# Attention and feed-forward layer on eight cores: the feed-forward moved a step later, a sequence's last halves of Q, K and V put beside its own attention, first loads in pieces, one span projected at first

## The reference, cut to what matters

```python
q, k, v = proj_heads(x, w_q), proj_heads(x, w_k), proj_heads(x, w_v)
scores = einsum('bhqd,bhkd->bhqk', q, k) / sqrt(64) + causal_mask
out = einsum('bhqk,bhkd->bhqd', softmax(scores), v)
x = layernorm(x + out @ w_o.T)
x_prev = x shifted by one token
xr = mu_r * x + (1 - mu_r) * x_prev
xk = mu_k * x + (1 - mu_k) * x_prev
ffn = sigmoid(xr @ W_r.T) * (square(relu(xk @ W_k.T)) @ W_v.T)
y = layernorm(x + ffn)
```

## Time and profile before

| | |
|---|---|
| median of 3 runs (lowest to highest) | 1367.66 us (1366.4 to 1368.92) |
| the profiled execution, whole | 1365.98 us |
| its span on the slowest core (of 8: 1347.0 to 1364.4) | 1364.4 us |
| TensorE busy | 1229.6 us, 90% |
| ScalarE, VectorE, GpSimd busy | 726.9 (53%), 653.4 (48%), 325.4 (24%) us |
| mean granted TensorE clock, as a share of 2.4 GHz | 0.975 |
| DMA: software queue (GpSimd), hardware queue (SP), share of 16 engines | 31.0%, 15.7% |

### The profile page before, as it was taken

How to read it: one execution, slowest core, us unless ns; L and a number is a source line. 1 busy time by engine, 2 the same in 40 slices (tenths; PEclk the granted TensorE clock), 3 DMA queues, 4 the chain that set the end, 5 groups by cost and what they waited for, 6 DMA issues and landing times.

```text
span 1364.4 us, 45398 instructions; the slowest of 8 cores (1347.0 to 1364.4 us)
## 1 busy us (share of the span) xinstructions
PE 1229.6 (90%) x18870; PEld 607.7 (45%) x18884; DVE 653.4 (48%) x1126; ACT 726.9 (53%) x1004; POOL 325.4 (24%) x440
## 2 busy tenths in 40 slices
PE   3999899989999598999997999999999969799776
PEld 1445354544454244444563545454444524344343
DVE  0005565456635164243275355636672615714696
ACT  1346555364656468666343254656565566877221
POOL 1002224211520115311124311631153110530141
PEclk9999999999999899999997999999999999999989
DMA  9977267964224722228643364345422471322302
GB/s 156 236 197 190 69 162 165 245 193 145 79 76 157 204 78 73 74 77 246 204 151 92 125 206 163 117 135 186 154 94 87 138 228 59 125 76 79 125 32 93
DMA packets 52617, 187.34 MB, mean 137 GB/s; under 512 B 11584, under 2 KB 27840, under 8 KB 36032
## 3 DMA queue, kind: packets, MB, share of 16 engines
q0 software_dynamic: 16416, 119.54, 31.0%
q1 hardware_dynamic: 36000, 64.89, 15.7%
HBM read 159.49 MB, written 31.46 MB: 140 GB/s over the span
## 4 chain that ended last, share of the span: by engine, by line
PE 74%; DMA 8%; DVE 5%; SPq 4%; ACT 4%; issue 3%; POOL 2%; DVEq 0%; POOLq 0%; ACTq 0%
PE DB L342 50%; PE S L709 9%; PE PVb L750 8%; SPq L820 4%; ACT P L724 4%; DMA rb<-rec 4%; PE DEN L773 3%; PE S L342 2%; DMA y<-x 2%; PE DB L507 2%; DMA ring<-wq 1%; DVE rec L812 1%; DMA ring<-wkf 1%; POOL QO L828 1%; POOL tmp L521 0%
## 5 line engine op out<-in xcount | busy, mean ns | idle before, releaser
L724 ACT ACTIVATE P<-S 128x1024 bf16<-128x1024 f32 (+3 forms) x640 | 535.4, 899 | 167.2 <-PE S L709 167.0
L709 PE MATMUL S<-QO,Kt 64*128 64x512 bf16 (+3 forms) x1280 | 187.1, 353 | 34.6 <-ACT P L724 33.5
L342 PE MATMUL DB<-xT,ring 128*32 128x512 bf16 (+1 forms) x2686 | 182.8, 380 | 21.3 <-DMA ring<-wq 20.9
L750 PE MATMUL PVb<-P,Vt 128*32 128x512 bf16 (+3 forms) x2560 | 179.0, 356 | 6.2 <-DVE u_s L810 3.7
L828 POOL TENSOR_TENSOR QO<-u_s,rb 128x512 bf16<-128x512 f32 x63 | 82.0, 1301 | 409.0 <-DMA rb<-rec 348.8
L734 DVE TENSOR_TENSOR P<-P,tri_s 128x512 bf16<-128x512 bf16 x128 | 63.7, 500 | 221.9 <-ACT P L724 221.8
L342 PE MATMUL DB<-ring,kact 128*32 128x512 bf16 x2312 | 143.9, 383 | 5.0 <-issue 2.8
L342 PE MATMUL DB<-ring,QO 128*32 128x512 bf16 (+1 forms) x1822 | 115.4, 387 | 22.9 <-POOL QO L828 20.8
L342 PEld LDWEIGHTS DB<-xT,ring 128*32 128x32 bf16 (+1 forms) x2688 | 97.0, 97 | 83.2 <-issue 25.5
L262 POOL DMA_DIRECT2D ring<-wscr x90 | 53.5, 594 | 336.1 <-PE S L709 184.2
L773 PE MATMUL DEN<-P,ones 128*32 128x256 bf16 (+1 forms) x2244 | 120.8, 270 | 8.5 <-DVE rec L812 8.4
(11 more groups left out here) (115 smaller groups left out, 1193.8 us busy)
## 6 DMA issues: line engine op xcount, KB each, us to landing
ring<-wscr POOLq DMA_DIRECT2D x90, 1024.0 KB, 6.5
rb<-rec SPq DMA_DIRECT2D x504, 32.0 KB, 2.9
x<-x SPq DMA_DIRECT2D x28, 512.0 KB, 8.7
wscr<-ring SPq DMA_DIRECT2D x14, 1024.0 KB, 10.1
y<-x SPq DMA_DIRECT2D x28, 512.0 KB, 7.6
xT<-xt POOLq DMA_DIRECT2D x6, 1024.0 KB, 12.5
ring<-wq POOLq DMA_DIRECT2D x2, 1024.0 KB, 25.5
kact<-xt POOLq DMA_DIRECT2D x2, 1024.0 KB, 18.6
```

What stands on the lines that cost most here:

```text
L342: mi = nc.tensor.matmul(out=b[r:r + w], lhsT=lhs[:, r:r + w], rhs=rhs, start=(cch == 0), stop=(cch == NCH - 1))
L709: mi = nc.tensor.matmul(out=sp[:, 512 * hh:512 * hh + n], lhsT=Kt[r, T * t + 128 * j:T * t + 128 * j + 128], rhs=QO[g % 2][r, SPW * t + q0 ...
L724: tok[("exp", k)] = SE.done(nc.scalar.activation(out=p3[:, :, 0:n], in_=s3, func=AF.Exp, bias=EXP_BIAS, scale=0.125), 0.14 + 2 * n / 1145)
L750: nc.tensor.matmul(out=PVb[r:r + 32, q0:SPW], lhsT=Vt[:, D * j + 128 * t + r:D * j + 128 * t + r + 32], rhs=P[:, p0 + h0:p0 + h0 + SPW - q ...
```

## The change

- `items_of` takes the place of `stages`. Step g now has F and RV of span g-2 (from step 2 on), then K of span g+1, O of g-1, Q of g+1, and T of g-1 in turns with V of g+1. Step 7 ends with F and RV of span 6.
- Of spans 3 and 7 only the first halves of K, Q, V (columns 0 to 511, pairs 0 to 3) are made in the step before; the last halves (`own_q`, `own_k`, `own_v`) are made in steps 3 and 7 beside the same span's attention. `s_unit` and `pv_unit` wait for K and V of the own span only on the diagonal.
- At first only span 0 is projected (`START`, 24 items: Q1 K1 K0 Q0 V0 V1), the halves K0, Q0, V0, V1 stay in the ring, and step 0 has span 1's 24 items.
- Dense items by step: 24 at first, then 24, 32, 44, 60, 8 (V of span 4 alone), 56, 56, 44, 68 and 32 behind.
- The first four half weights and xT of span 0 are loaded in four pieces of 512 KB of float32 each, with a semaphore for each piece; Q, K and F weights are laid out on the host so that a piece serves one item. `load_x` of span 0 waits until xT of span 0 has been read.
- Only span 1's xT lies in the kact tile; the others follow one another in the xT tile.
- `epilogue` copies on VectorE or ScalarE, whichever is free first; items are issued in halves in steps 3 and 7; some numbers of the planner change.

```diff
@@ -31,10 +31,10 @@
 NU = 3
 NB = 3
 LAG = 2
-XALT = (1, 5)
+XALT = (1,)
 DENSE = 1.75
 HALF = DENSE / 2
-AGE = 4.0
+AGE = 3.0
 class Ctr:
...
@@ -195,29 +197,44 @@
             return b
-        HALVES = {"K": [("wk", 0), ("wk", 1)], "Q": [("wq", 0), ("wq", 1)],
-                  "K0": [("wk", 0)], "K1": [("wk", 1)],
-                  "V": [("wv", 0), ("wv", 1)], "O": [("wo", 0), ("wo", 1)],
+        HALVES = {"K0": [("wk", 0)], "K1": [("wk", 1)], "Q0": [("wq", 0)], "Q1": [("wq", 1)],
+                  "V0": [("wv", 0)], "V1": [("wv", 1)], "O": [("wo", 0), ("wo", 1)],
                   "F": [("wkf", 0), ("wkf", 1)], "T": [],
                   "RV": [("wr", 0), ("wvf", 0), ("wr", 1), ("wvf", 1)]}
+        def items_of(g):
+            r, p, n = g - 2, g - 1, g + 1
+            def of(span, text):
+                return [(st, span) for st in text.split()]
+            def pairs(ts, side):
+                return [it for two in zip(ts, side) for it in two] + ts[len(side):] + side[len(ts):]
+            f, rv = (of(r, "F " * 8), of(r, "RV " * 16)) if r >= 0 else ([], [])
+            o, t = of(p, "O " * 8), of(p, "T " * 8)
+            k0, k1, q0, q1, v0, v1 = [of(n, st * 4) for st in ("K0 ", "K1 ", "Q0 ", "Q1 ", "V0 ", "V1 ")]
+            own_k, own_q, own_v = [of(g, st * 4) for st in ("K1 ", "Q1 ", "V1 ")]
+            if n == G:
+                return f + rv + own_q + o + pairs(t, own_k + own_v) + of(p, "F " * 8 + "RV " * 16)
+            if n % NSP == 0:
+                return f + own_q + rv + own_k + own_v + o + q0[:2] + pairs(t, q0[2:] + q1) + k0 + k1
+            if n % NSP == NSP - 1:
+                return f + rv + k0 + o + q0 + t[:2] + v0[:1] + t[2:4] + v0[1:2] + t[4:] + v0[2:]
+            return f + rv + k0 + k1 + o + q0 + q1 + pairs(t, v0 + v1)
         def stages(g):
-            p, n = g - 1, g + 1
-            if n == G:
-                return [("O", p), ("T", p), ("F", p), ("RV", p)]
-            if n % NSP == 0:
-                return [("O", p), ("Q", n), ("T", p), ("F", p), ("RV", p), ("K", n)]
-            if n % NSP == NSP - 1:
-                return [("K0", n), ("O", p), ("K1", n), ("T", p), ("V", n), ("F", p), ("RV", p), ("Q", n)]
-            first = [("K", n)] if g > 1 else []
-            return first + [("O", p), ("Q", n), ("T", p), ("V", n), ("F", p), ("RV", p)]
-        order = [("Q", 0), ("K", 0), ("V", 0), ("K", 2)]
+            return list(dict.fromkeys(items_of(g)))
+        START = ["Q1", "K1", "K0", "Q0", "V0", "V1"]
+        order = [(st, 0) for st in START] + [("K1", 1), ("Q1", 1)]
         for g in range(1, G):
             order += stages(g)
             if g + 1 < G and (g + 1) % NSP == 0:
-                order.append(("V", g + 1))
+                order += [("V0", g + 1), ("V1", g + 1)]
         order += [(st, G - 1) for st in ("O", "F", "RV")]
         uses = [w for st, _ in order for w in HALVES[st]]
...
@@ -245,6 +262,21 @@
             w, half = uses[n]
             slot = n % RING
             i = 2 * WNAMES.index(w) + half
+            if n < RING:
+                for q in range(4):
+                    if q == 1 and n == 0:
+                        load_xt(0)
+                    cast_at[0] = max(cast_at[0], GP.clock) + 2.0
+                    c = slice(1024 * q, 1024 * q + 1024)
+                    tok[("wq", n, q)] = tok[("w", n)] = GP.dma(wlq[n][q], GP.e.dma_start(
+                        out=ring[slot][:, c], in_=w_h[w][half, :, c]), cast_at[0] - GP.clock)
+                def keep():
+                    SY.need(*[tok[("wq", n, q)] for q in range(4)])
+                    tok[("scr", w, half)] = SY.dma(
+                        wst[slot], SY.e.dma_start(out=wscr[i], in_=ring[slot][:]), 6.0)
+                later(SY, 0.1, keep, tok[("w", n)])
+                return
             if n >= RING:
                 GP.need(wfree[n - RING], have(("scr",) + uses[n - RING]))
             if uses.index((w, half)) == n:
...
@@ -261,6 +293,8 @@
                 GP.need(have(("scr", w, half)))
                 t = GP.dma(wlc[slot], GP.e.dma_start(out=ring[slot][:], in_=wscr[i]), 8.0)
             tok[("w", n)] = t
+            if n == len(START) - 1:
+                load_xt(1)
         def take_weight():
             n = nxt[1]
...
@@ -293,11 +327,18 @@
         def load_xt(g):
-            if g < G:
+            if g == 0:
+                for q in range(4):
+                    cast_at[0] = max(cast_at[0], GP.clock) + 2.0
+                    c = slice(1024 * q, 1024 * q + 1024)
+                    tok[("xt", g)] = t = GP.dma(xtq[q], GP.e.dma_start(
+                        out=xT[g][:, c], in_=xt_h[g][:, c]), cast_at[0] - GP.clock)
+                    tok[("xtq", g, 2 * q)] = tok[("xtq", g, 2 * q + 1)] = t
+            elif g < G:
                 if g in XALT:
                     GP.need(tok[("vfmm", g - 3)] if g > 3 else None)
                 else:
-                    GP.need(tok[("xtmm", g - 2 if g - 1 in XALT else g - 1)] if g else None)
+                    GP.need(tok[("xtmm", g - 2 if g - 1 in XALT else g - 1)])
                 cast_at[0] = max(cast_at[0], GP.clock) + 10.0
                 tok[("xt", g)] = GP.dma(xts[g in XALT], GP.e.dma_start(out=xT[g], in_=xt_h[g]),
                                         cast_at[0] - GP.clock)
...
@@ -316,14 +357,19 @@
             s, t0 = x_rows(g, u)
             if g < G - 1:
-                SY.need(tok.get(("ystore", g - 1, u)))
+                SY.need(tok[("ystore", g - 1, u)] if g else tok[("xtmm", 0)])
             else:
                 SY.need(tok[("xtmm", g)] if u < 2 else tok[("omm", g - 1)])
-            tok[("x", g, u)] = SY.dma(xsl[u], SY.e.dma_start(out=xtile(g, u), in_=x_h[s, t0:t0 + 128, :]),
+            tok[("x", g, u)] = SY.dma(xsl[u + 4 * (g == G - 1)], SY.e.dma_start(out=xtile(g, u), in_=x_h[s, t0:t0 + 128, :]),
                                       6.0)
+        xt_reads = {}
         def xt_read(g, t):
+            xt_reads[g] = xt_reads.get(g, 0) + 1
+            if xt_reads[g] < 24:
+                return
             tok[("xtmm", g)] = t
             nx = g + 2 if g + 1 in XALT else g + 1
             if g not in XALT and nx not in XALT:
...
@@ -349,14 +395,19 @@
             def run():
                 b = dense_bank()
-                PE.need(have(("xt", g)), have(("w", wn)))
+                if wn < RING:
+                    PE.need(tok[("wq", wn, dch % 4)])
+                else:
+                    PE.need(have(("w", wn)))
                 for cch in range(NCH):
                     if cch == NCH // 2:
                         PE.clock += HALF
                         yield
-                    mi = dense_mm(banks[b], wtile(wn)[:, 512 * cch + 128 * (dch % 4): 512 * cch + 128 * (dch % 4) + 128],
-                                  xT[g][:, SPW * cch:SPW * cch + SPW], cch)
+                    PE.need(tok.get(("xtq", g, cch), have(("xt", g))))
+                    o = 1024 * (dch % 4) + 128 * cch
+                    mi = dense_mm(banks[b], wtile(wn)[:, o:o + 128], xT[g][:, SPW * cch:SPW * cch + SPW], cch)
                 t = PE.done(mi, HALF)
+                xt_read(g, t)
                 fill(t[2])
                 if which == "Q":
                     old = tok.get(("omm", g - 2))
...
@@ -388,12 +437,9 @@
                 bank_free[b] = tok[("V", g, half, u)] = evict(
                     t, Vt[:, D * i + 512 * half:D * i + 512 * half + 512], banks[b],
                     tok.get(("attn_mm", g - 1)) if g % NSP == 0 else None)
-                if u == 3:
-                    if rel:
-                        release_weight(wn, t)
-                    if half == 1:
-                        if g % NSP != NSP - 1:
-                            xt_read(g, t)
+                xt_read(g, t)
+                if u == 3 and rel:
+                    release_weight(wn, t)
             return run
         def part(g, u):
...
@@ -703,7 +750,7 @@
                 k = bn[0]
                 bn[0] += 1
                 sp = S[k % 2]
-                PE.need(tok.get(("exp", k - 2)), tok[("Q", g, t)], tok[("K", g, t)])
+                PE.need(tok.get(("exp", k - 2)), tok[("Q", g, t)], tok[("K", g, t)] if d >= 0 else None)
                 for hh in range(2):
                     r = slice(64 * hh, 64 * hh + 64)
                     mi = nc.tensor.matmul(
...
@@ -742,7 +789,7 @@
             for (g, t, j, k, d, q0, ts) in unit:
                 first, last = j == 0, j == 4 * (g % NSP) + 3
                 PE.need(have(("mask", k)) if d >= 0 else tok[("exp", k)],
-                        *[tok[("V", g, h, u)] for h in range(2) for u in range(4)],
+                        tok[("V", g, t // 4, d)] if d >= 0 else None,
                         tok.get("pvfree") if first else None)
                 p0 = 1024 * (k % NP)
                 for r in range(0, 128, 32):
...
@@ -806,9 +853,8 @@
             pn[0] += 1
             i, b = n % NU, n % NB
             fill(tm[2])
```

(59 more changed lines are left out.)

35 lines of the change are left out of this document (20 added, 15 removed).

## The result

The changed kernel takes 0.9856 of the time of the kernel before, with an interval of 0.9835 to 0.9877: about 1347.3 us against 1367. That is 20 us less, where 41 had been forecast. The direction and the range (1295 to 1352) held; the size was twice too large.

A forecast was written before the change was run, and what follows sets the result against it. The order of TensorE's work was taken to bound the kernel, its waits being short of dense work that could run. Work 1180.8 plus excess 142.3 gave 1323, with 1.6 more 1325 us; range 1295 to 1352.

The forecast's parts named there:

- The later feed-forward: From step 2, F and RV put at least 41 us ahead of O, so its waits of 8 to 11 us go.
- excess: A stage's length less its TensorE work at the prediction's prices; in sum 183.6 us before, 142.3 forecast.
- Own halves: Steps 3 and 7: 12 more items each beside attention; no cost in step 3, 10 us taken in step 7.
- x chain: From last residual to first O sum: layer norm, store and load of the x tile, 27 us, now between RV and O.
- the excess of a clean step: 7 to 9 us, dense work and attention mixed throughout; x chain's loss included; steps 2 and 6 given 9.
- The second rival: New order moves waits: attention alone in x chains, steps 2 and 4 to 7, 4 us each; 1345 us, chance 0.16.
- The start: First projections follow the loads, 7.7 us a half weight; excess 26 us against 23.8 before, bounds 18 to 38.
- Pieces: Start loads in quarters, 1.9 us each; first xT piece lands at 7.7, first TensorE work near 9 us.
- The ratio of 0.41: Page's 32% at 64 KB against 78% at 1 MiB; a piece would take 4.6 us, the start 65 us longer.
- The third rival: Start bound by loading: 3.9 us a piece instead of 1.9 costs 42 us, the whole gain; slower, chance 0.08.
- Step 7: Excess of 20 us against 29.9 before, with 68 dense items and 10 us taken for the hold.
- the hold: Attention held at pair 4's diagonal in step 7 while transposes wait for layer norm; 0 to 12 us, 10 taken.

The follow-up runs named there:

- two_spans_k: The changed kernel with spans 0 and 1 both projected at first, K of span 2 in step 0 and V of span 2 before O of span 0: ratio 0.9928.

## Why the prediction was right in sign and wrong in size

On core 2 the forecast missed by 18 us: 14 in steps 2 and 6, 12 at the start and 4 in step 7, less 12 in steps 0, 1 and 3. The first is a mechanism that the prediction had wrong, the second a term of the right kind that it sized too small. The 12 us in its favour are luck: no run explains them (up to 3 may be the difference between executions, as steps 0 and 1 show), and without them the miss would have been 30.

- **The later feed-forward: right.** The waits at O and for xk went, and undoing it alone costs 12 us. The steps that lost before (1, 3, 4, 7) have 50 us of excess instead of 99, against 54 forecast; that is both parts of the change together.
- **Own halves: the step that failed.** The prediction looked at steps 3 and 7, which get 12 items each, and gave steps 2 and 6, which lose 12 each, only 1.6 us for it, on the ground that they were clean before. They were clean with 56 items; with 44 the x chain and the transposes lie open. Half of this stood in the text (4 items for 12 us of a chain of 27); the step that failed was to say that its cost was "in the excess of a clean step" and to add nothing. The runs showed an excess of 15.6 instead of 9 in each of the two (mean of four cores), and that eight items ahead of O (K0 and K1) instead of four bring it to 5.6 to 6.8. In the trace after, the chain runs from the last residual at 312.7 to the first O sum at 335.9, 23 us (tile x on core 2: durations min/median/max, first and last start):

```profile
L719 DVE SCALAR_TENSOR_TENSOR x<-rbuf,x x5: 682/692/1767, 287.3 to 312.7; 128x512 f32<-128x512 f32 x5
...
L522 DVE TENSOR_TENSOR x<-DB,x x4: 691/692/693, 335.9 to 342.7; 128x512 f32<-128x512 f32 x4
```

  Measured, the own halves cost 7 to 8 us, and step 7, for which they were to bring most, is only 1 us better with them. The second rival named the mechanism (attention alone in each x chain) and gave 1345 us, 2 under what was measured. That nearness is chance: it put 4 us on each of steps 2 and 4 to 7 and nothing on the start, while steps 4 and 5 came out as forecast, steps 2 and 6 missed by 7 each and the start by 12.
- **Steps 2 and 6 and the row for a clean step.** The 7.4 us were read between round times. Without own halves the same steps have 6.0 and 5.6, so that price was fair, for 56 items with eight of them between RV and O.
- **The start: right in kind, at the upper bound in size.** 38.3 us of excess, where 26 was taken and 38 was the bound. The term that was mis-sized is a half weight's time: 7.7 us was taken throughout, and beside a copy in DRAM it was 10.8. The first two copies were faster than said (10.6 and 11.4 us against 15 to 20; the third and fourth took 13.7 and 15.6), which is the same thing seen from the other side: they took a third of the engines. The sixth load did wait for its slot, until 42.7, but that did not set its time: it then lay 30 us in its queue. The two copies held back give 4 to 5 us and whole loads 3.5; the rest of the 12 is not divided by any run.
- **Pieces.** They brought the first work forward by 10 us as forecast, and lost it again: whole loads end the start 3.5 us earlier. The Trainium skill's page "DMA: Bandwidth & Descriptors" (section Bandwidth) points the right way, in that smaller transfers move less here beside a copy, 0.97 against 1.28 MB in 10 us. The ratio of 0.41 that the prediction took from it lies between 64 KB and 1 MB, and the pieces have a quarter of the whole load's size, for which the page has no row; measured, it is 0.76 to 0.89 beside a copy, and 1.0 with the queue alone. The third rival's price, 3.9 us a piece, was not reached either; 10.8 us a half weight is 2.7 a piece. (Its time at 4.2 us a piece is 1374 by its own sum, not 1372.)
- **Step 7.** 23.8 against 20 forecast. The wait for the transposes came, with 3.6 us and not 10; the rest of the excess is attention alone before O and at the end. Of the hold and the x chain together, 4 us could be removed.
- **The signs named ahead.** First work at 10.8 (9 said); ring waits until 72.8 (60 said); end of V1 at 79.8, outside 62 to 75 and short of the 85 that was to refute the sum; no wait over 3 us for the scaled output at O: held; a wait of some 10 us for the transposes in step 7: 3.6, with attention held; a clock over 0.98 in steps 1 to 6: not in 2 and 6 (0.98 and 0.97), which are the two steps that missed.

## What to carry to other kernels

When work is moved from one stage to another, price the stage that gives it up as well: a stage is clean because of the items it has and where they stand, and its excess is no constant of the stage. Ask first which of the items that leave stood over a chain that something waits for. While loads bound a start, count every byte on every queue (copies out, reloads) before counting on smaller pieces, and follow a gain to the next stages before trusting it: 5, 3.5, 12 and 12 us won at the start (copies held back, whole loads, and the two kernels with two spans) were 1.6, 2.6, -0.6 and -10 at the beginning of step 2, and kernels with the same code differ there by up to 4 us. Where such a gain vanishes, look for one long wait before calling it given back.

## What the runs showed of the hardware

- With two loads of 512 KB before them, the four stores of y landed in 14.9 us (median) instead of 4.0.
- A copy of 1 MB from SBUF to DRAM on SP's queue, issued while loads with cast in pieces stood in GpSimd's queue, did not wait for them: the first two landed in 10.6 and 11.4 us. At 22 to 32 us SP's queue took 33.5% of the DMA engines' time, and the loads fell from 1.67 to 0.97 MB in 10 us.
- Eight transfers of 32 KB issued behind a load with cast of 1 MB on the other queue landed in 10.8 us (median, two_spans_k), against 3.0 over that kernel's 504.
- Waits of 1 to 2 us, three in a row between small transposes, were enough for the granted clock to fall: the 64 matmuls behind them took 6.44 us and not 3.63. On each side of them the clock was 1.00. In the kernel without own halves steps 2 and 6 have clocks of 1.00 and 0.99.
